# Ten more unread TensorE products per sample, in the second block inversion and at the end of the row

## The reference

```python
h = _layernorm(x) * (1 + ca) + sa
x = x + ga * attention_16_heads(h)            # causal softmax, head width 8
h = _layernorm(x) * (1 + cb) + sb
x = x + gb * moe_top2_of_8(h)                 # 128 -> 256 -> 128, relu
h = _layernorm(x) * (1 + ca) + sa             # layer 1's own gates from here
x = x + ga * gated_delta_net(h)
h = _layernorm(x) * (1 + cb) + sb
x = x + gb * ffn(h)                           # 128 -> 512 -> 128, tanh gelu, times the sum of the two router weights
```

```python
def step(S, inp):
    qt, kt, vt, bt, gt = inp
    S = S * jnp.exp(gt)[..., None, None]
    kv = jnp.einsum('bhk,bhkv->bhv', kt, S)
    delta = (vt - kv) * bt[..., None]
    S = S + jnp.einsum('bhk,bhv->bhkv', kt, delta)
    ot = jnp.einsum('bhk,bhkv->bhv', qt, S)
    return (S, ot)
```

## Time and profile before

| | us |
|---|---|
| median of three timed runs | 2636.61 (2632.77 to 2641.55) |
| the profiled execution, its own time | 2631.52 |
| its span, first to last instruction | 2629.8 |
| mean granted TensorE clock in it | 0.985 |

### The profile page before, as it was taken

The page is one execution under the profiler, slowest core; times in us unless marked ns, Lnnn a source line. Parts: engine busy times, 40 slices in busy tenths (PEclk is TensorE's granted clock), DMA queues, the critical chain, the costliest instruction groups (busy, mean ns, idle before and its releaser), DMA issues.

```text
span 2629.8 us, 64541 instructions
## 1 busy us (share of the span) xinstructions
PE 2335.7 (89%) x23582; PEld 1622.8 (62%) x23763; DVE 1751.6 (67%) x4602; ACT 1398.4 (53%) x3001; POOL 845.1 (32%) x589
## 2 busy tenths in 40 slices
PE   3899988999898998989989899898988989989898
PEld 2456865478554775547755477555774567655685
DVE  2557874787737776378754777557764678656786
ACT  0466445754448554485534845447444575446544
POOL 3136221542205421064301642115421253213621
PEclk8999999999999999999999999999999999999999
DMA  8301132011310103101130012301132011320113
GB/s 261 118 1 21 19 102 82 4 20 17 110 74 4 26 11 117 67 11 20 41 132 21 13 20 49 138 5 17 17 107 83 1 20 20 102 82 1 23 17 106
DMA packets 226957, 138.01 MB, mean 52 GB/s; under 512 B 173567, under 2 KB 209799, under 8 KB 219431
## 3 DMA queue, kind: packets, MB, share of 16 engines
q1 hardware_dynamic: 208870, 125.48, 16.8%
q10 hardware_dynamic: 17780, 8.39, 1.1%
HBM read 95.10 MB, written 38.71 MB: 51 GB/s over the span
## 4 chain that ended last, share of the span: by engine, by line
PE 50%; ACT 16%; DVE 14%; issue 8%; DMA 7%; SPq 3%; POOL 2%; ACTq 0%; DVEq 0%; POOLq 0%
PE bank L946 8%; PE bank L716 4%; PE bank L707 3%; PE bank L638 3%; PE bank L521 3%; PE bank L1049 3%; ACT arena L1680 3%; ACT arena L1681 3%; DVE small L1401 2%; ACT vq L1688 2%; DVE mx L1213 2%; PE bank L561 2%; PE bank L970 2%; PE bank L1070 2%; DMA vq<-k_rows 2%
## 5 line engine op out<-in xcount | busy, mean ns | idle before, releaser
L1349 DVE SCALAR_TENSOR_TENSOR arena<-bank,conv,arena 128x510 f32<-128x510 f32 x320 | 237.0, 747 | 45.2 <-ACT arena L1681 26.2
L1213 DVE TENSOR_REDUCE mx<-bank 128x2 f32<-128x768 f32 (+3 forms) x187 | 201.7, 1123 | 50.4 <-PE bank L562 49.1
L1976 POOL TENSOR_TENSOR arena<-upto,gk 128x1536 f32<-128x1536 f32 x32 | 88.2, 2757 | 450.0 <-DVE beta L1342 450.0
L1968 POOL TENSOR_TENSOR arena<-arena 128x511 f32<-128x511 f32 x160 | 201.9, 1274 | 56.1 <-DVE arena L1349 56.1
L521 PE MATMUL bank<-mask_k,ident_bf 128*128 128x512 bf16 x720 | 187.9, 385 | 13.5 <-issue 11.8
L1644 ACT ACTIVATE arena<-bank 128x384 f32<-128x384 f32 (+1 forms) x384 | 168.2, 545 | 46.5 <-PE bank L623 46.5
L778 PE MATMUL bank<-h_pad,arena 128*128 128x512 f32 x320 | 165.6, 615 | 28.7 <-DVE arena L1349 21.8
L561 PE MATMUL bank<-vq 128*128 128x128 bf16 (+3 forms) x532 | 121.4, 313 | 45.0 <-issue 22.4
L1401 DVE TENSOR_TENSOR small<-blk_tx,blk 96x1 f32<-96x1 f32 (+14 forms) x480 | 142.7, 297 | 17.5 <-DVE blk_tx L1403 0.8
L1665 ACT ACTIVATE arena<-bank,b1e 128x512 f32<-128x512 f32 x128 | 87.8, 686 | 116.8 <-PE bank L707 111.6
L1315 DVE SCALAR_TENSOR_TENSOR xs<-bank,comb,xs 128x128 f32<-128x128 f32 x256 | 72.0, 343 | 114.9 <-PE bank L716 114.2
(11 more groups left out here) (303 smaller groups left out, 5729.7 us busy)
## 6 DMA issues: line engine op xcount, KB each, us to landing
vq<-q_rows SPq DMA_DIRECT2D x18, 1024.0 KB, 8.1
vq<-k_rows SPq DMA_DIRECT2D x18, 1024.0 KB, 10.9
arena<-w_bounce SPq DMA_DIRECT2D x16, 1024.0 KB, 6.0
q_rows<-qkp SPq DMA_DIRECT2D x81, 128.0 KB, 2.4
k_rows<-qkp SPq DMA_DIRECT2D x81, 128.0 KB, 2.4
arena<-wv_rows SPq DMA_DIRECT2D x8, 768.0 KB, 10.3
ogt<-wv_rows SPq DMA_DIRECT2D x8, 768.0 KB, 11.8
t_bounce<-blk_tx SPq DMA_DIRECT2D x32, 192.0 KB, 2.1
```

Of the source, the lines that this page charges most:

```text
L1213: V.reduce_max(dst, unit_scores(u), AX.X).then_inc(s_max, 1)
L1349: ins = V.scalar_tensor_tensor(a[:, k:T], ps[:, 0:T - k], conv[:, n, 3 - k:4 - k], a[:, k:T], ALU.mult, ALU.add)
L1968: G.tensor_tensor(acc[:, n % 4, 1:T], acc[:, n % 4, 1:T], second(n)[:, 0:T - 1], ALU.add).then_inc(taps_added, 1)
```

## The change

In the second inversion (c = 1) the list becomes the third one's: one product more before stage 4, one more before stage 6, and two before stage 7, where there were none. The first inversion stays. At the row's end six are added in bank 5: two before the wait of the product j = 2, three behind that product, and one before the wait of the product j = 3. That is ten per sample, 80 in all. No other engine's instructions change.

```diff
@@ -894,7 +894,7 @@
                         for s in range(8):
                             if c < 2:
-                                keep_warm(3, {3: 4, 4: 2, 6: 2}.get(s, 0))
+                                keep_warm(3, ({3: 4, 4: 3, 6: 3, 7: 2} if c else {3: 4, 4: 2, 6: 2}).get(s, 0))
                             elif c == 2:
@@ -1092,8 +1092,11 @@
                     for j in range(FT):
                         if j >= 2:
+                            keep_warm(5, 4 - j)
                             pe.wait_ge(f_sb, at(b, f_sb, j - 1))
                         mm(f_bank(j)[:, :], w1[:, j * P:(j + 1) * P], h_t[:, :], start=True, stop=True).then_inc(f_ps, 1)
+                        if j == 2:
+                            keep_warm(5, 3)
                         scores(b, 1, 2 + j)
```

## The result

The changed kernel takes 2650.02 us in the median of twenty runs (2638.70 to 2667.64); the kernel before takes 2635.10 in the twenty beside them (2626.85 to 2647.70). The ratio is 1.0049, with a 95% interval of 1.0035 to 1.0063: slower, and above the range of the prediction. The profiled execution of the changed kernel takes 2655.98 us, 24.5 more than the profiled one of before; its median is 14.9 more, so the trace shows somewhat more of the loss than a usual run has.

What follows compares the result with a forecast made beforehand. TensorE, nearly at full clock, was taken as the bound. 4.75 + 1.73 - 4.65 - 2.93 = -1.1 us on 2631.52 gave 2630.4, carried over to a 2635.5 us median; range 2629 to 2643.5.

Steps and rivals of the forecast that it cites:

- What is won: Row's ends and second inversions regain full clock: 4.65 us taken whole, and 2.93, half of 5.87.
- the stop of a microsecond stays: Stage 5, samples 3 and 5: stops of 0.97 and 1.24 us remain, a reason to count only half the inversion gain.
- rival 3: Stages 6 and 7 and fourth L1096: products are paid and win nothing, +7.4 us, 2644.0; chance 0.12.
- chance shift of the low pieces in stretches that the change leaves alone: Unedited stretches: low-clock pieces may move by chance, adding a little to the 0.08 for slower.
- rival 1: Row's ends and inversions all keep the clock, the third inversion's list cited as support: -4.0 us, 2632.6; chance 0.18.
- Row's end: L1096 to L567: 17.07 us at clock 1.00 in all eight samples; price +1.73 us, gain 4.65.
- Second inversion, direct price: Stage 3's products to stage 7: four added products lengthen 6.05 us to 6.87, 0.82 per sample.
- Cover: Wait at L1021 hides part of the second inversion's price, none in even samples; exposed price +4.75 us in all.
- ScalarE's wait before stage 7: Second inversion, L1801 waiting on TensorE's stage 6: wait to rise from 0.37 to about 0.6 us.
- Inversions kept at the full clock: Second inversion and after, samples 3 and 5: of 5.87 us lost to low clock, half, 2.93, is won.
- The Trainium skill's rule: TensorE clock: short waits with work between cost no clock, so filling them would win nothing; doubted because of falls seen.

Runs made afterwards that it cites:

- placed changed kernel: Changed kernel with TensorE's code shifted against its 256-instruction blocks by short products and by cutting unread products in even samples; 2627.72 us, ratio 0.9976 to the kernel before.
- placed kernel before: Kernel before, without the ten products, its code shifted likewise with cuts of its own so that block edges lie alike; 2630.65 us, ratio 0.9978.
- row's end alone: Kernel before plus only the six unread products of the row's end, second inversion unchanged; 2643.15 us, ratio 1.0019 to the kernel before.

## Why the prediction was wrong

**The failed step** stands under "What is won" and in the sum. I had the two stops of the earlier trace rows in front of me, "released by nothing that the profile shows", took them as fixed ("the stop of a microsecond stays"), and priced the ten products as work and cover alone. An edit of TensorE's program has a second effect, that everything behind it moves against the code blocks, and the sum had no term for it. Measured, that term is about the whole of the 14.9 us: 1.0049 as built, 0.9976 against 0.9978 once both kernels are placed. None of the five rivals was this mechanism; rival 3 had the right sign of the result and the wrong reason, and the "chance shift of the low pieces in stretches that the change leaves alone" got a small part of the 0.08 for slower. A clue was in the trace of before: its third inversion, which rival 1 holds to have no such stop, has one of 0.23 to 0.50 us in stage 6 in all four even samples (1.7 us in the view of waits above).

- **Row's end: right in its mechanism.** 17.01 to 17.02 us against 17.07 expected, all three falls gone. A product costs (17.01 - 16.85) = 0.16 us per sample here, not 0.216. The net gain is 3.4 us against 2.92 in my sum.
- **Second inversion, direct price: right.** From the first unread product of stage 3 to stage 7 it takes 592.16 - 585.08 = 7.08 us in sample 2, counted with the first product, which the earlier trace rows leave out: 6.86 without it, against 6.87. Even samples' stretches grow by 0.84 to 0.87.
- **Cover: wrong.** I took the even samples for uncovered, because the view of waits counts no wait at L1021 there, so 4.75 us in all. Timeline, sample 2, TensorE's products and VectorE's differences that they read, of the kernel before and of the changed one:

```profile
590.97 3.18 DVE L1435 SCALAR_TENSOR_TENSOR arena<-bank,neg_dec,vq 128x128 f32<-128x128 f32 x12
...
592.14 3.23 PE L1021 MATMUL bank<-arena 128*128 128x128 f32 x24
```
```profile
598.32 3.18 DVE L1438 SCALAR_TENSOR_TENSOR arena<-bank,neg_dec,vq 128x128 f32<-128x128 f32 x12
...
600.11 2.97 PE L1021 MATMUL bank<-arena 128*128 128x128 f32 x24
```

The same 24 rows took 3.23 us and now take 2.97. They began 1.2 us behind VectorE's first difference and now begin 1.8 us behind it; so before they were most likely paced by VectorE, in pieces too short to be listed as waits. With the way up to them (592.14 - 584.00 = 8.14 against 600.11 - 592.16 = 7.95) that is 0.45 us of cover in a sample without one listed. The net price is 0.33 us per even sample (above), and 0.16 per odd one: 70.10 in the mean of the placed changed kernel's odd samples over both stretches, 69.95 in the placed kernel before. Times four each it is 2.0 us, not 4.75.
- **ScalarE's wait before stage 7**: I expected some 0.6 us for L1801 (now L1804). It is 0.58 in sample 2 and 1.15 in sample 1, where a stop in stage 5 and the low clock behind it come in as well.
- **Inversions kept at the full clock: wrong.** I took half of 5.87 us as won. In its place the odd samples stop in all four, and all but sample 3 lose the clock, and the even ones, which had kept their clock, lost it in all four behind the third inversion: 12.1 us that no line of my text reaches.
- **The Trainium skill's rule** (TensorE: Matmul & The Clock Gate, "What's actually happening") by which waits this short cost no clock, and which I let stand as part of a rival, is contradicted again: falls follow stops of about a microsecond here. The sizes are in the last section.

What is shown and what is not: that the place of the code makes and removes these stops, and that the place is worth up to 40 us, is shown by kernels with the same loop. That the fetch of the block is what TensorE waits for rests on the count and on the nearly constant delay of 2.2 to 2.9 us behind the transfer; nothing in the trace names it as the releaser. Why a transfer starts within some 1.7 us of the edge in most crossings and some 2 us or more after it in others stays open, and with it why one place gives a stop in some turns and not in others; so my counts of stops, each from one execution, carry some chance, and the medians do not. Also open is the first stretch (row's end to inversion 1), whose sums lie between 1385.6 and 1407.1 us in these kernels by pieces at the lower clock that I did not trace to a cause.

## What to carry to other kernels

When an edit of an engine with dense short instructions moves the time in stretches that it does not touch, look for idle time that ends with "issue", count instructions between such places, and compare with the sizes in the instruction queue: if they recur by one block's length, measure the kernel again with a few instructions put into a long wait ahead of the loop, before judging the edit. Judge an edit of a per cent or less by its kernel at two or three such places: here the place alone moved the time by 1.5%, the edit as built by 0.5%, and the edit with its code placed by nothing that can be told. And an engine that no view lists as waiting can still be paced by another: compare the length of the same group of instructions in both traces.

## What the runs showed of the hardware

- TensorE's code comes by 16,384 bytes (199 transfers, 3.26 MB), by my count one for each 256 instructions. Where 256 instructions take 4 to 5 us, TensorE stops for 0.2 to 1.8 us at edges whose transfer began late, and goes on 2.2 to 2.9 us behind the transfer's start in all 88 stops.
- What the clock did behind a stop went with the stop's length, but not by length alone. In the profiled executions of these fourteen kernels the third inversion has 27 such stops within its groups of small products. Behind the 13 of 0.23 to 0.58 us the clock held in all (29.35 to 29.37 us to the fourth inversion); behind the 14 of 0.85 to 1.48 us it fell to 1.2 GHz in 13, for 7 to 10 us (31.8 to 32.6 us). Two more falls, in the row's end alone, stand behind stops between two groups, which the trace lists as a wait for ScalarE. In the first and second inversions the line is not so clean: behind the 23 stops of 0.82 to 1.84 us the clock fell in all, but behind the 27 of 0.48 to 0.76 us in 16. So in the third inversion a stop of half a microsecond costs itself, and one of a whole 2.5 to 3.3 us more; in the others half a microsecond can do.
